# Cross-attention of a decoder layer: operand stacks filled by SBUF copies instead of a trip through DRAM, and softmax sums inverted in their own PSUM bank

## The reference

```python
x = x + self_attention(layernorm(x), wq, wk, wv, wo)       # 16 heads, window 256
x = x + cross_attention(layernorm(x), ctx, ctx, gamma)
x = x + expert_mix(layernorm(x), ...)                      # 16 experts, top-k tokens of each

def cross_attention(q, v, gamma):                          # channel attention: 8 heads of 32 rows
    qh = q.reshape(B, 8, 32, 512); kh = vh = v.reshape(B, 8, 32, 512)
    qk = einsum('bhdq,bhdl->bhql', qh, kh) / sqrt(32)      # 512 x 512 for each head
    sm = softmax(qk, axis=-1)
    ret = einsum('bhql,bhdl->bhdq', sm, vh)
    return gamma * ret.reshape(B, 256, 512)
```

## Time and profile before

| | us |
|---|---|
| median of three runs (2817.76 to 2822.01) | 2818.88 |
| the profiled execution's own time | 2815.54 |
| its span, first to last instruction | 2813.8 |
| first layer norm and self-attention, up to PE's last matmul there | 0 to 2012 |
| cross-attention | 2012 to 2615 |
| expert mix | 2615 to 2813.8 |

### The profile page before, as it was taken

One profiled execution on the slowest core, in us unless ns is written; L12 is line 12 of the kernel. 1 busy time (PEld: TensorE's weight loads), 2 busy tenths in 40 slices (PEclk: granted clock), 3 DMA queues, 4 the chain that ended last, 5 costly groups with the idle time before them and its releaser, 6 DMA issues. The chain is left out here.

```text
span 2813.8 us, 38435 instructions
## 1 busy us (share of the span) xinstructions
PE 2639.5 (94%) x13448; PEld 1978.8 (70%) x13448; DVE 1737.7 (62%) x3567; ACT 990.8 (35%) x2474; POOL 862.5 (31%) x698
## 2 busy tenths in 40 slices
PE   3699999999999999999999999999599999999795
PEld 2488888888888888888888888888444444444573
DVE  7466656666555565556665666666467777675557
ACT  2222222322222232222223222222257777776220
POOL 2111111322111142111123211211258887777100
PEclk9999999999999999999999999999889999999797
DMA  8512111332111232112222213210367777762003
GB/s 312 188 56 95 61 60 61 108 107 86 61 60 60 102 124 75 60 61 81 99 75 90 75 61 105 76 60 31 124 182 188 185 187 185 190 188 62 20 1 120
DMA packets 165098, 290.08 MB, mean 103 GB/s; under 512 B 11568, under 2 KB 78128, under 8 KB 162864
## 3 DMA queue, kind: packets, MB, share of 16 engines
q1 hardware_dynamic: 164912, 287.65, 32.7%
HBM read 194.81 MB, written 92.27 MB: 102 GB/s over the span
## 5 line engine op out<-in xcount | busy, mean ns | idle before, releaser
L439 PE MATMUL pj<-xnt,whi 128*128 128x512 f32 x2048 | 704.2, 405 | 16.2 <-DMA xnt<-xt_scratch 16.2
L519 ACT ACTIVATE pr<-sc,nmx 128x128 f32<-128x128 f32 (+1 forms) x512 | 211.1, 417 | 934.7 <-DVE nmx L591 934.7
L394 POOL TENSOR_TENSOR qt<-rot,swp 128x512 f32<-128x512 f32 x128 | 166.1, 1298 | 1127.4 <-DVE swp L572 1127.4
L439 PEld LDWEIGHTS pj<-xnt,whi 128*128 128x128 f32 x2048 | 385.6, 188 | 108.5 <-DMA xnt<-xt_scratch 16.6
L990 DVE TENSOR_REDUCE xnmx<-xsc 128x1 f32<-128x512 f32 x512 | 336.7, 685 | 162.6 <-PE xsc L810 159.6
L439 PE MATMUL pj<-xnt,wlo 128*128 128x512 f32 x1024 | 398.7, 389 | 0.0
L780 POOL TENSOR_TENSOR xprt<-xprt 128x512 f32<-128x512 f32 x256 | 320.3, 1280 | 116.2 <-PE xob L830 87.5
L436 PE MATMUL pj<-whi,xnt 128*128 128x512 f32 x1024 | 351.7, 405 | 0.0
L932 ACT ACTIVATE xprt<-xst 128x512 f32<-128x512 f32 x512 | 290.6, 595 | 112.1 <-PE xst L819 108.8
L570 DVE TENSOR_TENSOR rot<-pj,trig 128x512 f32<-128x512 f32 x256 | 177.0, 691 | 226.8 <-PE pj L439 226.8
L591 DVE TENSOR_REDUCE nmx<-sc 128x1 f32<-128x128 f32 (+1 forms) x512 | 158.6, 352 | 177.3 <-PE sc L465 172.8
(11 more groups left out here) (185 smaller groups left out, 4344.1 us busy)
## 6 DMA issues: line engine op xcount, KB each, us to landing
xnt<-xt_scratch SPq DMA_DIRECT2D x64, 1024.0 KB, 8.0
x_scratch<-xio SPq DMA_DIRECT2D x64, 512.0 KB, 3.5
xio<-x_scratch SPq DMA_DIRECT2D x48, 512.0 KB, 4.1
qst<-sq_scratch SPq DMA_DIRECT2D x96, 256.0 KB, 5.1
kst<-sk_scratch SPq DMA_DIRECT2D x96, 256.0 KB, 5.7
xt_scratch<-parts SPq DMA_DIRECT2D x16, 1024.0 KB, 4.7
sq_scratch<-qp SPq DMA_DIRECT2D x32, 512.0 KB, 8.0
sk_scratch<-kp SPq DMA_DIRECT2D x32, 512.0 KB, 4.8
```

The source lines that it names most:

```text
L394: nc.gpsimd.tensor_tensor(qk["QK".index(kind)][h][:, :, :].rearrange("p b n -> p (b n)"), rot[r % 2][:, :], swp[r % 2][:, :], ALU.add).the ...
L439: last = nc.tensor.matmul(bank[:, :], wpart[:, w, i * HD:(i + 1) * HD], moving, start=(k == 0), stop=(k == 3 * CB - 1))
L519: nc.scalar.activation(pr[:, a % 4, lo:hi], SC[a % 2][:, lo:hi], ACT.Exp, bias=nmx[:, a % 4, t:t + 1], accum_out=rsum[:, a % 4, t:t + 1]). ...
```

## The change

- **The context is given twice**: as `ctx_in`, and transposed on the host as `ctx_t` (tile, column in block, block, row). `load_values` loads the second straight into `vt` (now three buffers, 256 KB a tile). `values`, `v_evac` and the bank `VB` go.
- **Stacks by copies**: `write_queries`, `write_keys`, `read_stacks` and both DRAM scratch tensors go. `spread` copies from `qp` and `kp` (now two buffers each) straight to the stacks, 3 x 2 x 4 = 24 DMAs a tile, of 32 partitions x 2 KB (64 KB) each. It has the gates that the read had, and in addition waits for both rests. ACT's rounding of tile m now waits for the copies of tile m - 2.
- **Inverse sums**: ACT takes the logarithm of the sums and exponentiates its negative (`log_of_sums`, `inverse_of_sums`), DVE makes one Newton step in the sums' own bank (`newton`, `newton_end`), of which there are now two. `sums_evac`, `sums_by_query`, `one_over_sums`, `repeat` and `inverses` go. Gamma is applied in `output_evac`.
- **Order**: `weigh` moves from a step's end to after its second pair, `sums` from after the second pair to the end of steps 0 and 2. SP's loop issues `spread(n + 2)`, `load_values(n + 2)`, context, x and the maximum rows. `RING` goes from 5 to 6. `AHEAD = 6` and `STACKS = 3` stay.
- **The second layer norm's rstd** is computed by DVE alone, from an integer seed with four Newton steps, without ACT's square root.

```diff
         AHEAD = 6
-        RING = 5
+        RING = 6
         STACKS = 3
...
             def load_context(m):
                 if m >= 4:
-                    sp.wait_ge(s_vt, m - 3)
                     sp.wait_ge(s_klo, m - 3)
...
-            def write_queries(m):
+            def load_values(m):
+                if m >= 3:
+                    sp.wait_ge(s_pv, CB * (m - 2))
+                sp.dma_start(vt[:, m % 3, :, :], ctx_t[m]).then_inc(s_vt[m % 3], 16)
+
+            def spread(m):
                 sp.wait_ge(s_qlo, m + 1)
-                sp.dma_start(sq[m % 2].rearrange("h p d -> p h d"), qp[:, :, :].bitcast(F32)).then_inc(s_qw, 16)
-
-            def write_keys(m):
                 sp.wait_ge(s_klo, m + 1)
-                sp.dma_start(sk[m % 2].rearrange("h p d -> p h d"), kp[:, :, :].bitcast(F32)).then_inc(s_kw, 16)
-
-            def read_stacks(m):
-                sp.wait_ge(s_qw, 16 * m + 16)
-                sp.wait_ge(s_kw, 16 * m + 16)
                 if m >= STACKS:
                     sp.wait_ge(s_ts, 16 * (m - STACKS) + 16)
-                qv = sq[m % 2].rearrange("h (j r) d -> h r j d", j=XPT)
-                kv = sk[m % 2].rearrange("h (j r) d -> h r j d", j=XPT)
                 for c in range(PARTS):
                     rows = slice(XD * c, XD * (c + 1))
-                    sp.dma_start(qst[m % STACKS][rows, :, :].bitcast(F32), qv[c // 2]).then_inc(s_st[m % STACKS], 16)
-                    sp.dma_start(kst[m % STACKS][rows, :, :].bitcast(F32), kv[c % 2]).then_inc(s_st[m % STACKS], 16)
+                    for stack, parts, part in ((qst, qp, c // 2), (kst, kp, c % 2)):
+                        for j in range(XPT):
+                            src = parts[m % 2][XD * j:XD * (j + 1), part, :]
+                            sp.dma_start(stack[m % STACKS][rows, j, :].bitcast(F32),
+                                         src.bitcast(F32)).then_inc(s_st[m % STACKS], 16)
...
                 if tile(n + 2):
-                    read_stacks(n + 2)
-                if tile(n + 3):
-                    write_queries(n + 3)
-                    write_keys(n + 3)
+                    spread(n + 2)
+                    load_values(n + 2)
...
                 if h == 0 and q == 0:
-                    pe.wait_ge(s_st[m % STACKS], 16 * 2 * PARTS * (m // STACKS + 1))
+                    pe.wait_ge(s_st[m % STACKS], 2 * COPIES * (m // STACKS + 1))
...
-                    if i == 1:
-                        middle(s // CB, s % CB)
-                if 0 <= s - 1 < STEPS:
-                    weigh(s - 1)
+                    if i == 1 and s % CB == 2 and tile(s // CB + 1):
+                        max_transposes(s // CB + 1)
+                    if i == 1 and 0 <= s - 1 < STEPS:
+                        weigh(s - 1)
+                if s % CB in (0, 2) and tile(s // CB - 1):
+                    sums(s // CB - 1, s % CB // 2)
...
             def q_round(m):
                 act.wait_ge(s_qn, m + 1)
-                act.wait_ge(s_qw, 16 * m)
-                nc.scalar.activation(qp[:, 0, :], xn[:, :], ACT.Copy).then_inc(s_qhi, 1)
+                if m >= 2:
+                    act.wait_ge(s_st[(m - 2) % STACKS], 2 * COPIES * ((m - 2) // STACKS + 1))
+                nc.scalar.activation(qp[m % 2][:, 0, :], xn[:, :], ACT.Copy).then_inc(s_qhi, 1)
...
+            def log_of_sums(n):
                 act.wait_ge(s_su, 2 * n + 2)
-                act.wait_ge(s_sq, n)
-                nc.scalar.activation(ssb[:, :], SU[:, :], ACT.Copy).then_inc(s_se, 1)
+                act.wait_ge(s_new, 2 * n)
+                nc.scalar.activation(rin[:, :], SU[n % 2][:, :], ACT.Ln).then_inc(s_log, 1)
+
+            def inverse_of_sums(n):
+                act.wait_ge(s_log, n + 1)
+                nc.scalar.activation(rin[:, :], rin[:, :], ACT.Exp, scale=-1.0).then_inc(s_inv, 1)
...
-            WORK = {(0, 0): ((k_round, 3),), (0, 1): ((repeat, -2),), (0, 2): ((v_evac, 0),), (1, 0): ((output_evac, -1),),
-                    (1, 1): ((normed, 4),), (1, 3): ((q_round, 4),), (2, 2): ((max_round, 1),), (2, 3): ((sums_evac, -1),)}
+            WORK = {(0, 0): ((k_round, 3),), (0, 2): ((output_evac, -1),), (1, 1): ((normed, 4),), (1, 3): ((q_round, 4),),
+                    (2, 2): ((max_round, 1),), (3, 0): ((log_of_sums, -1),), (3, 2): ((inverse_of_sums, -1),)}
...
+            def newton(n):
+                dve.wait_ge(s_inv, n + 1)
+                nc.vector.scalar_tensor_tensor(SU[n % 2][:, :], SU[n % 2][:, :], -1.0, rin[:, :],
+                                               ALU.mult, ALU.mult).then_inc(s_new, 1)
+
+            def newton_end(n):
+                dve.wait_ge(s_new, 2 * n + 1)
+                nc.vector.scalar_tensor_tensor(SU[n % 2][:, :], SU[n % 2][:, :], 2.0, rin[:, :],
+                                               ALU.add, ALU.mult).then_inc(s_new, 1)
...
-            WORK = {(0, 1): ((statistics, -3),), (0, 2): ((mean_and_variance, -3),), (2, 0): ((output, -2),),
-                    (2, 2): ((max_rest, 1),), (3, 3): ((one_over_sums, -1),)}
+            WORK = {(0, 0): ((statistics, -3),), (0, 1): ((newton, -2),), (0, 2): ((mean_and_variance, -3),),
+                    (0, 3): ((newton_end, -2),), (1, 1): ((output, -2),), (2, 2): ((max_rest, 1),)}
```

More of the change, by code:

```diff
@@ L643, in cross_attention @@
         KM = KS + 2
+        COPIES = 16 * PARTS * XPT
         AHEAD = 6
[L645 removed]
+        RING = 6
         STACKS = 3
@@ L648, in cross_attention @@
         gam = sb("gam", [P, 1], F32)
-        tmp = sb("rs_tmp2", [P, 2, TILES], F32)
+        var = sb("var2", [P, TILES], F32)
+        seed = sb("seed2", [P, TILES], I32)
+        half = sb("half2", [P, TILES], F32)
         rstd = sb("rstd2", [P, TILES], F32)
@@ L673, in cross_attention @@
         OB = pb("xob")
-        SU = pb("xsu")
-        VB = pb("xvb")
+        SU = [pb(f"xsu{i}") for i in range(2)]
         s_shift = sem("x_shift")
-        s_gam, s_var, s_sqrt, s_step = sem("x_gam"), sem("x_var"), sem("x_sqrt"), sem("x_step")
+        s_gam, s_step = sem("x_gam"), sem("x_step")
         s_xi = [sem(f"x_xi{i}") for i in range(6)]
@@ L829, in weigh @@
                     rows = slice(XD * h, XD * (h + 1))
-                    last = nc.tensor.matmul(OB[rows, :], vt[:, n % 2, c, rows], prt[s % RING][:, h, :],
+                    last = nc.tensor.matmul(OB[rows, :], vt[:, n % 3, c, rows], prt[s % RING][:, h, :],
                                             start=(c == 0), stop=(c == CB - 1))
@@ L835, in sums @@
                 pe.wait_ge(s_add, XPT * (2 * n + k + 1))
-                if k == 0:
-                    pe.wait_ge(s_se, n)
+                if k == 0 and n >= 2:
+                    pe.wait_ge(s_on, n - 1)
                 for h in range(XPT):
                     rows = slice(XD * h, XD * (h + 1))
-                    last = nc.tensor.matmul(SU[rows, :], ones[:, :], prt[(CB * n + 2 * k) % RING][:, h, :],
+                    last = nc.tensor.matmul(SU[n % 2][rows, :], ones[:, :], prt[(CB * n + 2 * k) % RING][:, h, :],
                                             start=(k == 0), stop=(k == 1))
                 last.then_inc(s_su, 1)
-            def values(n):
-                pe.wait_ge(s_ci[n % 4], 16 * (n // 4 + 1))
-                if n >= 2:
-                    pe.wait_ge(s_ri, n - 1)
-                for c in range(CB):
-                    last = nc.tensor.transpose(VB[:, c * P:(c + 1) * P], cin[:, n % 4, c * P:(c + 1) * P], ident[:, :])
-                last.then_inc(s_vt, 1)
             def max_transposes(n):
@@ L855, in max_transposes @@
                 nc.tensor.transpose(MX[0:XPT * CB, 0:P], nmx[:, n % 2, :], ident[:, :]).then_inc(s_mt, 1)
-            def sums_by_query(n):
-                pe.wait_ge(s_se, n + 1)
-                pe.wait_ge(s_vte, min(n + 2, TILES))
-                pe.wait_ge(s_on, n)
-                for q in range(CB):
-                    last = nc.tensor.matmul(VB[:, q * XPT:(q + 1) * XPT], ssb[:, q * P:(q + 1) * P], ident[:, 0:P:XD],
-                                            start=True, stop=True)
-                last.then_inc(s_sq, 1)
-            def inverses(n):
-                pe.wait_ge(s_rr, n + 1)
-                pe.wait_ge(s_vte, min(n + 3, TILES))
-                for q in range(CB):
-                    last = nc.tensor.transpose(VB[:, q * P:(q + 1) * P], rrep[:, q, :], ident[:, :])
-                last.then_inc(s_rt, 1)
-            def middle(n, c):
-                if c == 0:
-                    if tile(n - 1):
-                        sums(n - 1, 0)
-                    if tile(n):
-                        values(n)
-                if c == 1 and tile(n - 2):
-                    inverses(n - 2)
-                if c == 2:
-                    if tile(n - 1):
-                        sums(n - 1, 1)
-                    if tile(n + 1):
-                        max_transposes(n + 1)
-                if c == 3 and tile(n - 1):
-                    sums_by_query(n - 1)
```

(16 more changed lines are left out.)

64 lines of the change are left out of this document (22 added, 42 removed).

## The result

The changed kernel takes 3197.4 us (median of 4 runs, 3194.4 to 3199.7) beside 2818.6 of the kernel before (4 runs): 1.134 times as long, 95% interval [1.132, 1.136]. The forecast was slower, which holds, but 2970 with a range up to 3050 was 227 us too little. All times here are of undisturbed executions; only the profiled execution of run 6 was a slowed one (3279 us), so of its profile local rows alone are read.

The account below looks back on a forecast made before the run. It took PE's own list to bound the kernel before, and the new copies to make PE wait. Landing 13.2, work 7.6 and clock 1.8 gave a 22.6 us tile; 29 x (22.6 - 17.18) less 2 gave 2970 us, range 2905 to 3050.

Parts of the forecast that it names:

- The mechanism: Cross-attention tile: 24 copies spaced 0.47 us, landing some 2 us after last issue, PE waiting about 5 us before step 2.
- T: Start of a tile, when the previous tile's last transposed score has ended and SP can begin filling a stack.
- the price of an issue: SP's queue: each of a stack's 24 copies was taken to cost 0.475 us, within bounds of 0.37 and 0.64.
- Copies inside SBUF are as dear as the maximum rows: Rival on SP's queue: 0.64 us an issue, landing T + 17.0, tile 26.4 us, total some 3085; chance 0.20.
- T + 13.2: Forecast time of the stack's landing: 23 issues of 0.475, 2.1 us to land, 0.1 for each semaphore.
- The tables: Rival in ACT's step 3: logarithm and exponential evict each other's tables, two 1.28 us loads a tile, 75 more; chance 0.04.
- The clock: PE behind each landing: 5.3 us wait drops clock to 1.2 GHz, 3.6 us at half speed, losing 1.8 us a tile.
- The ends: Outside the gated tiles: about 4 us later before the first tile, 6 us back at the last, together -2.
- the path behind it: PE from the stack's landing through steps 2 and 3 to the last transposed score: 7.6 us at full clock.
- the removed work: Sums by query, value and inverse transposes taken off PE: 1.7 us a tile, at most 2.2 with ACT's late starts.
- its other side: Faster rival: issues of 0.24 us or less leave PE's list as bound, 15.3 us a tile, about 2757; chance 0.09.

Follow-up runs that it names:

- run 6: Changed kernel with the shared logarithm/exponential table set loaded once and 130 small filler matmuls on PE ahead of each gated stack's wait: 3118.2 us, ratio 1.107.
- run 2: Changed kernel with its 24 copies a tile reading a DRAM scratch tensor instead of SBUF, same size, count and target: 3071.8 us, ratio 1.090.
- run 1: Changed kernel with the table set holding both logarithm and exponential loaded once ahead of the stage: 3129.0 us, ratio 1.110.
- run 3: Changed kernel with 115 small filler matmuls on PE ahead of its wait for each gated stack: 3175.6 us, ratio 1.127.
- Run 11: Kernel before the change, only the stack's six reads made twelve, heads 0 and 1 first, a semaphore for each half: 2804.5 us, ratio 0.995.
- run 5: Changed kernel with stacks filled through DRAM as before the change, and the shared table set loaded once: 2833.6 us, ratio 1.006.
- 8: Changed kernel with stacks through DRAM, shared table set loaded once, and the old PE order of `sums` and `weigh`: 2809.6 us, ratio 0.997.
- run 9: Changed kernel with stacks through DRAM, one table load, new PE order, and stack reads in halves with a semaphore each: 2779.0 us, ratio 0.986.
- run 4: Changed kernel with stacks filled through DRAM as before the change, all else as changed, table loads included: 2923.6 us, ratio 1.037.

## Why the prediction was wrong

**The mechanism was right.** Copies spaced evenly from the tile's start, the last landing 2 us after its issue, one wait of PE before the scores of step 2 put down to `kst`, low-clock matmuls behind it: all there. PE ended its steps 0 and 1 at T + 7.8 where its clock was up, as forecast (7.9), and near T + 9.0 where it had fallen behind ACT's pause. Its wait was 8.3 us in the mean (6.7 to 10.1) instead of 5.3.

**The step that failed is the price of an issue.** "I take 0.475, because in shape ... the copies are nearest to the loads": it is 0.633, the upper bound, and the rival "Copies inside SBUF are as dear as the maximum rows", given 0.20, is what happened. The stack was there at T + 16.9 in the mean, forecast T + 13.2: 3.7 us a tile. The maximum rows were the only rows of before with both ends in SBUF, and that, by run 2, was the likeness that counted. That the landing would be at T + 17.0 by 0.64 stands in the prediction. (Its totals for the dear copies are 4 to 5 us too high: by its own sum 0.64 gives 3081 and 0.55 gives 3020.) Even the dear copies with the tables would have given only some 3156; the rest is in the next paragraphs.

**The tables came on top.** "A load of ACT's function tables takes 1.28 us; two a tile" was given 0.04; it is the case in all tiles. Run 1 measures 68 us against the 75 worked out. The only reason in view for the low chance is the sentence on a table set that holds both. The Trainium skill ("ScalarE: Activation LUTs", section "Table sets: the hidden batching unit") has one load for a logarithm and an exponential behind it; the trace of after has two, and only with that set loaded by hand (run 1) does none remain in the loop. That a set exists is no evidence that the kernel uses it.

**The clock cost more than 1.8 us.** From landing to last transposed score it is 8.0 us with the clock up (run 3: 10.1 less the pause of 2.13), where 7.6 was forecast, and 10.4 with it down (run 1, mean): 2.4 us. The low stretch lasts up to 6.1 us there, and not the 3.9 counted from 2059.22 in the earlier trace rows. That count starts late: in the trace of before PE is busy 2.00 of 2.00 us at 0.50 already from 2056 to 2058.

**The ends.** Forecast -2 us; the account shows +23.5 and +16.8, of which one tile's 12.3 belongs to the sum: +28. Of the 23.5, 3.4 us stand before the stage, whose first DVE operation comes at 2021.02 instead of 2017.59, and no part of the change is shown to cause them. Another 19.7 us stand in the distances of the first four stacks, which are 15.9, 20.7 and 26.0 us instead of 11.8, 14.4 and 16.8: the forecast counts the gated tiles alone, but the first stacks are 24 copies each as well. The `rstd` chain takes 8.7 us (2021.02 to 2029.68) instead of 4.1, near what was forecast. Three of its steps take some 1.8 us, the first of which the kernel before has too:

```profile
2021.02 1.80 DVE L933 TENSOR_SCALAR var<-mv 128x32 f32<-128x32 f32 x1 [3.48 <-PEq L237]
```

Together, in means over the 28 tiles: the landing 3.7, the path behind it 0.4, the tables 2.1, the clock 0.6 make 6.8 of the 6.86 us by which the tile was mis-sized; 29 x 6.86 + 30 is the 229 us between 2970 and the profiled execution. The size of the ends was not tested by itself.

**What the prediction didn't see at all** is that the removed work could buy nothing as long as the stack came at the old time. It says so for steps 0 and 1, but takes the kernel before as bound by PE's list. Run 11 shows that it waited for its stacks too, and runs 5 and 8 that the change without its copies stands within 0.6% of before. The 15.3 us a tile of its other side, PE's list as the bound, was reached by no run; the nearest is 16.02 (run 9).

## What to carry to other kernels

Where a buffer is freed late in one turn and wanted early in the next, write the turn down as a loop of release, refill, work up to the next release: an engine that is 99% busy may be doing work that only fills this loop's wait, and to take it away gives nothing until the refill comes sooner or in parts. When an operation is not in the trace, price it by the row that has the same two ends (here both in SBUF), even if its size and shape differ, and multiply by the count before choosing. A move within an order has a sign only in relation to what is late: measure it again when the wait has gone.

## What the runs showed of the hardware that was not expected

- An issue on SP's queue costs 0.633 us when source and target are both in SBUF and 0.465 us when the source is in DRAM, for the same 64 KB, shape and target (after, run 2).
- Pauses of PE of 2.13 to 2.16 us were followed by the lower clock, in the tile shown for 6.3 us, in all 29 tiles of run 4, but behind 19 of 29 pauses of the same length in after, where a longer wait stands in each tile too. Of the waits of 1.18 to 1.95 us in run 5, 1 of 25 was.
- Copies whose issue on SP's queue took over 0.8 us (up to 1.9) instead of 0.59 had a packet of the instruction queue beside them or in the microsecond before: 10 of 10 in after, 39 of 40 in run 3, 42 of 42 in run 6. It happens without filler, and more often with it.
- The first three DVE operations of the stage, on 128 x 32 elements, took 1.80 to 1.82 us, where their neighbours of that size take 0.19 (after, 2021 to 2029). Two of them are on integers, but the same two operations in expert mix take 0.55 and 0.23 us (L1282, L1283), so integers are not the reason.
